# An attention and expert kernel on one core: the first pair's keys and values brought together by one-hot products on TensorE, not by gathers

## Chip, cores and metric

One core of a Trainium2 chip. The metric is the device time of one execution in microseconds. The kernel before took 506.49 us (median of three runs, 504.88 to 506.61).

## The reference

The input `x` is 2048 tokens of 128 channels. Cut to what matters here:

```python
h = layernorm(x) * (1 + ca) + sa
q, k, v = split(h @ qkv_w.T + qkv_b)                  # 16 heads of 8 channels
scores = sigmoid(sigmoid(relu(h @ r_w1.T + r_b1) @ r_w2.T + r_b2))
top_idx = top_k(scores of a head over the tokens, 819)  # k_keep = int(2048 * 0.4)
attn = q @ k.T / sqrt(8), all but the 819 kept keys of the head at -1e30
x = x + ga * (softmax(attn) @ v)
h = layernorm(x) * (1 + cb) + sb
x = x + gb * (the one of 8 experts that the router picks, for each token)
```

Each head keeps 819 of 2048 tokens as keys, and which ones is known only at run time. So the kernel has to bring the kept keys and values of a head together.

## The kernel before, in words

Engines and their queues: TensorE (`pe`), VectorE (`dve`), ScalarE (`act`), GpSimd (`pool`) and SyncE (`sp`) each run their own program in the order written, tied by semaphores.

**Start.** Layer norm, products for queries, keys, values and router scores. VectorE searches each head's threshold in 11 rounds (L977 to L987), in whose gaps TensorE makes keys and values (`KV`, copied by ScalarE at L755 and written to `kv_dram` by SyncE). Then VectorE computes for each token and head the place of the token among the kept ones (L992 to L1023), TensorE turns the table (L1454), and VectorE takes it from PSUM (L1025) and splits it in a low part and a key (L1027 to L1033).

**Lists.** Heads are worked in 8 pairs. The list of pair `i` is the row numbers of its kept keys and values in `kv_dram`. `columns(i)` (L1037) and `onehot(i)` (L1049) of VectorE make one-hot tables, `index_mm(i)` (L1459) multiplies them in 16 products, ScalarE copies (`copy_codes`), `row_to_partition(i)` (L1473) turns, and `index(i)` (L1057) writes the row numbers. `AHEAD = 5` lists, those of pairs 0 to 4, are made in front, one after another. Lists 5, 6 and 7 are made in the loop: `LIST_BESIDE` is {11: 5, 15: 6, 19: 7}; their columns are made by GpSimd (L651), their products stand in chunks 11, 15 and 19 and their row turn in the chunk behind.

**Gathers.** With a list, GpSimd issues 13 indirect DMAs of 128 rows each (L586) into `G`. For pair 0 they are split in 7 and 6, and VectorE prepares the keys (`prep`, L1071): bias added, then three bf16 parts whose sum is the key, in six copies (48 rows) beside each other in `KS`. TensorE turns them (L1600, L1609) into `KT`, where the keys of a head lie side by side, head 0 on partitions 0 to 63 and head 1 on 64 to 127. For the other pairs GpSimd does the same (L591 to L634) and TensorE turns in `turn_k` (L1523), in chunk n with n % 4 == 1.

**Lead and loop.** The tokens' queries are cut in 4 chunks of 512, so there are 32 chunks in all. A score unit (`score_unit`, L1505) is one 128-query by 410-key product, whose maximum VectorE takes from one of three PSUM banks (L1107). Of each chunk there are 16. `LEAD = 28` units, ordered by `unit_order()`, run ahead of the loop; each chunk of the loop issues 16 units of later chunks. The row maxima of a chunk, split in three parts, are turned (L1534), copied (L790) and sent by SyncE into the query rows (`m_rows`, L499); no chunk can start before its own have landed. In chunk n, TensorE makes scores (L1569) in 7 steps, ScalarE the exponentials (L823), TensorE weighs the values (L1585, L1593). After `m_rows(0)` SyncE issues the load of all experts (`WE`, two DMAs of 2 MB, L512), which waits for the lists in front since they use the same memory.

**End.** Second layer norm, router, and 23 tiles of expert work.

## Time and profile before

| | |
|---|---|
| median of three runs | 506.49 us |
| the profiled execution | 507.32 us, of which the span of the trace 505.4 us |
| TensorE busy | 435.7 us (86%) |
| VectorE busy | 399.7 us (79%) |
| ScalarE busy | 312.4 us (62%) |
| GpSimd busy | 221.9 us (44%) |
| mean granted clock of TensorE | 0.906 |

A reader sees in such a profile how long each engine had work in hand, what its idle time waited for, and a chain of work followed back from the end. A granted clock of 1.0 stands for 2.4 GHz, 0.5 for 1.2 GHz.

### The profile page before, as it was taken

To read this page: it belongs to the slowest core of one execution; us is meant where nothing else is said; L and a number is where in the kernel's file an instruction comes from. 1 tells how busy PE (TensorE), PEld (TensorE's weight loads), DVE (VectorE), ACT (ScalarE), POOL (GpSimd) and SP (SyncE) were. 2 spreads that over 40 slices of the span, in tenths; PEclk is the share of its full clock that TensorE was granted. 3 is DMA by queue.
4 is the path that set the end of the run, shared out by engine and by line. 5 is a ranking of instruction groups with operands and counts; after the bars stand their busy time and mean duration, and the time that the engine had idled before them with its cause. 6 is when DMAs were issued, how large, how long until landed. Compare 5 with 4: busy or idle time off the path is not lost.

```text
span 505.4 us, 9690 instructions
## 1 busy us (share of the span) xinstructions
PE 435.7 (86%) x3335; PEld 188.9 (37%) x3335; DVE 399.7 (79%) x1081; ACT 312.4 (62%) x486; POOL 221.9 (44%) x304
## 2 busy tenths in 40 slices
PE   3666558989999999999999999999999998599782
PEld 3332442223333333333323233323333225289672
DVE  8788958869988988789769958888888996746451
ACT  2435200367877877687667748787787874068562
POOL 3300287573505367358437625435000600177775
PEclk9888555599999999899869969999999999899997
DMA  8032610630100100010010000001000032021210
GB/s 255 1 123 66 161 13 6 227 116 5 35 2 7 35 4 6 9 32 3 6 35 3 7 24 15 5 5 36 1 2 2 2 100 68 10 77 53 63 31 23
DMA packets 20209, 21.15 MB, mean 42 GB/s; under 512 B 5740, under 2 KB 15792, under 8 KB 20160
## 3 DMA queue, kind: packets, MB, share of 16 engines
q1 hardware_dynamic: 14689, 16.13, 10.5%
q0 software_dynamic: 5168, 4.00, 3.8%
q8 instruction: 27, 0.44, 0.3%
q10 hardware_dynamic: 303, 0.40, 0.2%
q14 instruction: 22, 0.18, 0.1%
HBM read 14.42 MB, written 7.27 MB: 43 GB/s over the span
## 4 chain that ended last, share of the span: by engine, by line
PE 61%; DVE 20%; issue 7%; ACT 4%; DMA 4%; POOL 3%; POOLq 0%; SPq 0%; DVEq 0%; ACTq 0%
PE OP L1585 18%; PE ST L1569 12%; DVE tile_max L1107 8%; PE SC L1517 6%; PE SC L1515 5%; PE ST L1738 2%; PE OP L1593 2%; PE ST L1542 2%; DMA KV<-rows_dram,owner 2%; DVE PR L977 2%; PE SC L1727 2%; PE ST L1548 2%; POOL out L721 2%; ACT PR L823 1%; PE ST L1469 1%
## 5 line engine op out<-in xcount | busy, mean ns | idle before, releaser
L1107 DVE TENSOR_REDUCE tile_max<-SC 128x1 f32<-128x410 f32 (+1 forms) x512 | 268.5, 576 | 47.4 <-PE SC L1515 44.0
L823 ACT ACTIVATE PR<-ST 128x1024 f32<-128x1024 f32 (+1 forms) x224 | 210.7, 960 | 52.0 <-PE ST L1569 51.8
L586 POOL DMA_INDIRECT G<-kv_dram,idx x104 | 106.6, 1025 | 142.4 <-ACT PR L823 79.6
L1569 PE MATMUL ST<-QS,KT 51*128 51x512 bf16 (+1 forms) x416 | 116.8, 400 | 1.6 <-DMA QS<-MT 1.2
L1585 PE MATMUL OP<-PR,VS 128*32 128x512 f32 x768 | 107.8, 635 | 0.1
L1515 PE MATMUL SC<-KT,QS 48*128 48x410 bf16 x256 | 79.6, 366 | 4.0 <-ACT KT L794 1.9
L1569 PEld LDWEIGHTS ST<-QS,KT 51*128 51x128 bf16 (+1 forms) x416 | 31.7, 96 | 55.4 <-issue 41.9
L1517 PE MATMUL SC<-KT,QS 48*128 48x409 bf16 x128 | 47.1, 368 | 3.4 <-DVE tile_max L1107 0.2
L1519 PE MATMUL SC<-KT,QS 48*128 48x358 bf16 x128 | 43.5, 340 | 0.7 <-DVE tile_max L1107 0.7
L712 POOL DMA_INDIRECT KV<-rows_dram,owner x23 | 24.1, 1047 | 40.8 <-DVE owner L1351 34.1
L1515 PEld LDWEIGHTS SC<-KT,QS 48*128 48x128 bf16 x256 | 19.5, 95 | 46.1 <-DVE tile_max L1107 30.6
L1517 PEld LDWEIGHTS SC<-KT,QS 48*128 48x128 bf16 x128 | 12.0, 94 | 56.0 <-DVE tile_max L1107 42.9
L641 POOL TENSOR_TENSOR XN<-OTS,REC 128x128 f32<-128x128 f32 x14 | 5.5, 412 | 56.5 <-DVE REC L1130 52.8
L878 ACT ACTIVATE HT<-ST,mod_col,one_cb 128x128 f32<-128x128 f32 x23 | 10.5, 457 | 30.2 <-PE ST L1718 30.2
L790 ACT ACTIVATE MT<-ST 24x128 bf16<-24x128 bf16 x32 | 8.5, 267 | 31.6 <-PE ST L1548 16.5
L721 POOL DMA_INDIRECT out<-PR,owner x23 | 23.8, 1035 | 7.0 <-issue 5.8
L1369 DVE COPY PR<-WE 128x512 f32 x23 | 10.4, 453 | 20.6 <-PE ST L1738 20.5
L1738 PE MATMUL ST<-PR 128*128 128x128 f32 x184 | 24.9, 278 | 0.8 <-ACT PR L889 0.4
L1520 PE MATMUL SC<-KT,QS 48*128 48x51 bf16 x128 | 24.7, 193 | 0.0
L1727 PE MATMUL SC<-HT,PR 128*128 128x128 f32 x184 | 24.3, 276 | 0.0
L1585 PEld LDWEIGHTS OP<-PR,VS 128*32 128x32 f32 x768 | 15.4, 110 | 21.1 <-issue 15.1
L1738 PEld LDWEIGHTS ST<-PR 128*128 128x128 f32 x184 | 22.3, 191 | 1.5 <-issue 1.1
(269 smaller groups left out, 568.6 us busy)
## 6 DMA issues: line engine op xcount, KB each, us to landing
kv_dram<-KV SPq DMA_DIRECT2D x4, 512.0 KB, 2.9
WE<-in_w_fc SPq DMA_DIRECT2D x1, 2048.0 KB, 9.3
WE<-in_w_proj SPq DMA_DIRECT2D x1, 2048.0 KB, 14.7
G<-kv_dram,idx POOLq DMA_INDIRECT x104, 2.4
q_parts_dram<-QP SPq DMA_DIRECT2D x3, 512.0 KB, 3.7
QS<-q_parts_dram SPq DMA_DIRECT2D x16, 96.0 KB
X<-in_x SPq DMA_DIRECT2D x4, 256.0 KB, 5.9
QS<-q_parts_dram SPq DMA_DIRECT2D x16, 64.0 KB
```

Of the source, the lines that this page charges most:

```text
L586: pool.indirect_dma_start(G[:, i % 2, slot_of(s), :], None, kv_dram, bass.IndirectOffsetOnAxis(ap=idx[:, i, s:s + 1].bitcast(U32), axis=0) ...
L721: pool.indirect_dma_start(out[0], bass.IndirectOffsetOnAxis(ap=owner[:, n:n + 1].bitcast(U32), axis=0), YS[:, n, :], None, bounds_check=L ...
L823: nc.scalar.activation(PR[:, k, 0:cols], ST[:, (KSTEPS * n + k) % 2, 0:cols], ACT.Exp, scale=float(D) ** -0.5).then_inc(exp_done, 1)
L1107: v.tensor_reduce(tile_max[:, n % 2, at_col:at_col + 1], bank(RING_AT["unit", u])[:, 0:410 - f], AX.X, ALU.max).then_inc(s_reduced, 1)
L1515: last = mm(to[:, 0:410], q, KT[rows, i % 2, 0:410], start=True, stop=True)
L1517: last = mm(to[:, 0:409], q, KT[rows, i % 2, 410:KEEP], start=True, stop=True)
L1519: mm(to[:, 0:358], q, KT[rows, i % 2, 410:768], start=True, stop=True)
L1520: last = mm(to[:, 358:409], q, KT[rows, i % 2, 768 + GAP:KTCOLS], start=True, stop=True)
L1569: last = mm(ST[:, at_step % 2, 512 * e:512 * e + 512], KT[rows, i % 2, P * tile:P * tile + P], QS[rows, i % 2, CHUNK * c:CHUNK * (c + 1)], ...
L1585: last = mm(OP[32 * g:32 * g + 32, :], VS[:, i % 2, tile, :], PR[:, k, 512 * e:512 * e + 512], start=first, stop=False, skip_group_check=True)
L1727: last = mm(SC[:, b, P * c:P * c + P], WFC[:, b, P * c:P * c + P], HT[:, P * n:P * n + P], start=True, stop=True)
L1738: last = mm(ST[:, b, 0:E], R2[:, b, P * c:P * c + P], WPROJ[:, b, P * c:P * c + P], start=(c == 0), stop=(c == 3))
```

## The change

Pair 0 has no list and no gathers any more. GpSimd adds the bias to the keys and values of heads 0 and 1 for all 2048 tokens in SBUF and splits them in three bf16 parts (`split0`, into `parted`). VectorE compares, for each of the 16 token tiles and both heads, the 896 slot numbers (`column`, written by GpSimd at the start) with each token's place; this gives a one-hot row for each token (`hot`, a ring of 7). TensorE multiplies parts by one-hot rows, 64 products in all, summed over the tiles in two PSUM banks: each kept token's parts arrive in its slot's column. A product with `repeat` puts the parts in the six copies that `KT` wants, and seven products with `add_parts` turn and add the parts of the values.

`AHEAD` is 3. List 1 is made at the beginning of the lead by VectorE (columns, one-hot, index) with its products between units 3 to 7, list 2 at its end, with columns by GpSimd. Lists 3 to 7 are made in the loop: `LIST_BESIDE` is {3: 3, 7: 4, 11: 5, 15: 6, 19: 7}. The units run in natural order, so that chunk 0 has its 16 maxima after 16 units and not after 20. The keys of pair 1 are turned at step 5 of chunk 1 and not at step 2. The expert load waits for the products instead of five lists. The table of constants has 160 more columns. The diff, cut:

```diff
-TURN_AFTER = 7
-ODD_AFTER, ODD_TURN_AFTER = 7, 9
-AHEAD = 5
+TURN_AFTER = [0, 14] + [7] * (NP - 2)
+AHEAD = 3
+HOTS = 7
 LIST_BESIDE = {NQ * (i - 3) + 3: i for i in range(AHEAD, NP)}
...
-ORDER = unit_order()
+ORDER = [(n, qt, f, e) for n in range(NCH) for qt in range(4) for f in range(2) for e in (1, 0)]
...
-            sp.wait_ge(columns_ready, AHEAD)
+            sp.wait_ge(columns_ready, 1)
+            sp.wait_ge(hot_used, NT)
             for n, w_part in enumerate((w_fc, w_proj)):
...
+            def numbered(e, first, last, tile):
+                nc.gpsimd.tensor_tensor(column[:, e, P * first:P * last].rearrange("p (k j) -> p k j", j=P),
+                                        block[:, tile:tile + last - first, :].to_broadcast([P, last - first, P]),
+                                        lane.to_broadcast([P, last - first, P]), ALU.add).then_inc(pool_step, 1)
+                pool.wait_ge(pool_step, next_step())
+            numbered(0, 0, BLOCKS, 0)
+            numbered(1, 0, BLOCKS - 1, 1)
+            numbered(1, BLOCKS - 1, BLOCKS, 0)
+            nc.gpsimd.tensor_copy(repeat16[:, :], cc("repeat")).then_inc(pool_step, 1)
...
+            nc.gpsimd.tensor_copy(add_parts16[:, :], cc("add_parts")).then_inc(pool_step, 1)
...
+            nc.gpsimd.memset(parted, 0.0).then_inc(pool_step, 1)
...
+            nc.gpsimd.memset(parted[:, :, :, KROWS:SROWS], 1.0).then_inc(pool_step, 1)
...
+            def split0():
+                pool.wait_ge(kv_ready, NT // 2)
+                pool.wait_ge(bias_in, 16)
+                shape = [P, NT, 2, 2 * D]
+                nc.gpsimd.tensor_tensor(biased, KV[:, :, 0:4 * D].rearrange("p t (e c) -> p t e c", e=2),
+                                        BG[:, 0:1, 0:2, :].to_broadcast(shape), ALU.add).then_inc(part_step, 1)
+                pool.wait_ge(part_step, 1)
+                nc.gpsimd.tensor_copy(parted[:, :, :, 0:16], biased).then_inc(part_step, 1)
+                pool.wait_ge(part_step, 2)
+                nc.gpsimd.tensor_tensor(rest1, biased, parted[:, :, :, 0:16], ALU.subtract).then_inc(part_step, 1)
...
-            gathers(0, range(EARLY), gathered_early)
-            gathers(0, range(EARLY, STEPS), gathered_late)
-            gathers(1)
-            prep(1)
-            prep_v(1)
...
+            columns(2)
+            pool.wait_ge(columns_late, 3)
+            gathers(1)
+            prep(1)
+            prep_v(1)
             for i in range(2, NP):
                 if AHEAD <= i + 1 < NP:
                     columns(i + 1)
...
-            for i in range(AHEAD):
-                copy_codes(i)
-            act.wait_ge(ktr_odd, 1)
-            nc.scalar.activation(KT[64:128, 0, :], OP[:, :].bitcast(BF16)[64:128, 0:KTCOLS], ACT.Copy)\
-                .then_inc(kt_odd, 1)
+            act.wait_ge(hot_used, NT)
+            nc.scalar.activation(turned0[:, 0:512], SC[:, 0, :], ACT.Copy).then_inc(turned0_ready, 1)
+            act.wait_ge(kt0_done, 1)
+            nc.scalar.activation(KT[:, 0, 0:512], ST[:, 1, 0:512], ACT.Copy).then_inc(kt0_ready, 1)
+            copy_codes(1)
...
-            v.tensor_copy(place_int[:, :], MP[:, 0:CT]).then_inc(dve_step, 1)
+            v.tensor_copy(places, MP[:, 0:CT]).then_inc(dve_step, 1)
+            dve.wait_ge(dve_step, next_step())
+            dve.wait_ge(init_pool, 1)
+            for t in range(NT):
+                if t >= HOTS:
+                    dve.wait_ge(hot_used, t - HOTS + 1)
+                for e in range(2):
+                    v.tensor_scalar(hot[:, t % HOTS, e, :], column[:, e, :], places[:, H * t + e:H * t + e + 1], None,
+                                    ALU.is_equal).then_inc(hot_ready, 1)
+            v.tensor_copy(place_int[:, :], places).then_inc(dve_step, 1)
...
+            dve.wait_ge(hot_used, NT)
+            v.tensor_copy(turned0[:, 512:KTCOLS], SC[:, 2, 0:KTCOLS - 512]).then_inc(turned0_ready, 1)
...
+            dve.wait_ge(kt0_done, 1)
+            v.tensor_copy(KT[:, 0, 512:KTCOLS], ST[:, 1, 512:KTCOLS]).then_inc(kt0_ready, 1)
...
-            for i in range(AHEAD):
-                columns(i)
-                onehot(i)
-                if i >= 1:
-                    index(i - 1)
-            index(AHEAD - 1)
+            columns(1)
+            onehot(1)
...
+            units(0, 8)
+            index(1)
+            units(8, LAST[0] + 4)
+            onehot(2)
+            units(LAST[0] + 4, LEAD)
+            index(2)
...
-            for i in range(AHEAD):
-                index_mm(i)
-                row_to_partition(i)
+            pe.wait_ge(parted_ready, 1)
+            for t in range(NT):
+                of_t = NT // CHUNKS * (t % CHUNKS) + t // CHUNKS
+                for half, (c0, c1) in enumerate(((0, 512), (512, KTCOLS))):
+                    for e in range(2):
+                        if half == 0:
+                            pe.wait_ge(hot_ready, 2 * t + e + 1)
+                        last = mm(SC[64 * e:64 * e + 64, 2 * half, 0:c1 - c0], parted[:, of_t, e, :],
+                                  hot[:, t % HOTS, e, c0:c1], start=(t == 0), stop=(t == NT - 1), skip_group_check=True)
+                last.then_inc(hot_used, 1)
+            pe.wait_ge(turned0_ready, 2)
+            mm(ST[:, 1, 0:512], repeat16[:, :], turned0[:, 0:512], start=True, stop=True)
+            mm(ST[:, 1, 512:KTCOLS], repeat16[:, :], turned0[:, 512:KTCOLS], start=True, stop=True).then_inc(kt0_done, 1)
...
+            index_ready(1)
+            for u in range(3, 8):
+                if u < 6:
+                    index_part(1, [range(0, 5), range(5, 10), range(10, NT)][u - 3])
+                score_unit(u)
+            row_to_partition(1)
+            for k in range(7):
+                last = mm(ST[:, 1, 32 * k:32 * k + 32], turned0[:, P * k:P * k + P], add_parts16[:, :], start=True, stop=True)
...
-                    if k == 2 and n % NQ == 1 and n // NQ + 1 < NP:
+                    if k == (5 if n == 1 else 2) and n % NQ == 1 and n // NQ + 1 < NP:
                         turn_k(n // NQ + 1)
```

## Rows read from the trace of the kernel before

**Rows 1.** The page: clock row of the 40 slices, and the chain's shares by engine
```profile
PEclk9888555599999999899869969999999999899997
...
PE 61%; DVE 20%; issue 7%; ACT 4%; DMA 4%; POOL 3%; POOLq 0%; SPq 0%; DVEq 0%; ACTq 0%
```
**Rows 2.** Windows: stretch, its length, busy of each engine, clock, DMA share, GB/s
```profile
65.00:70.00 5.00, 4.10 (x47) 3.50 (x45) 2.59 (x4) 0.43 (x2) 4.05 (x3) 0.50 0.08 10
...
50.95:76.34 25.39, 14.09 (x171) 11.57 (x170) 18.60 (x34) 3.51 (x9) 13.25 (x11) 0.52 0.36 81
76.34:92.65 16.31, 14.00 (x43) 3.95 (x44) 14.92 (x36) 1.18 (x2) 12.47 (x13) 0.50 0.07 8
92.65:105.70 13.05, 11.73 (x58) 2.88 (x58) 9.79 (x25) 6.79 (x8) 6.32 (x16) 0.59 0.92 324
```
**Rows 3.** The chain in order of time, 45 to 108 us: start, length, what
```profile
55.90 2.06 PE SC L1469 x16
...
68.71 1.00 POOL G L586
...
76.91 3.53 DVE tile_max L1107 x7
...
99.78 5.91 DMA QS<-MT
105.74 0.39 PE ST L1569
```
**Rows 4.** Timeline of ScalarE: the copy of a pair's keys, pairs 2 to 6
```profile
148.60 0.91 ACT L794 ACTIVATE KT<-SC 128x896 bf16<-128x896 bf16 x1
...
186.86 0.91 ACT L794 ACTIVATE KT<-SC 128x896 bf16<-128x896 bf16 x1
...
228.46 0.91 ACT L794 ACTIVATE KT<-SC 128x896 bf16<-128x896 bf16 x1
...
272.73 0.91 ACT L794 ACTIVATE KT<-SC 128x896 bf16<-128x896 bf16 x1
...
317.07 0.91 ACT L794 ACTIVATE KT<-SC 128x896 bf16<-128x896 bf16 x1
```
**Rows 5.** Timeline, 30 to 56 us: the last copy of keys and values
```profile
39.01 0.60 ACT L755 ACTIVATE KV<-SC 128x512 f32<-128x512 f32 x1 [1.46 <-PE SC L1424]
```
**Rows 6.** Timeline at 227 us, and the durations of L1121 (minimum, median, maximum)
```profile
227.07 1.69 POOL L659 TENSOR_TENSOR B<-key_of,C 128x896 f16<-128x896 f16 x1
...
227.65 1.13 DVE L1121 TENSOR_TENSOR NM<-NM 128x8 f32<-128x8 f32 x1
...
L1121 DVE TENSOR_TENSOR NM<-NM x32: 153/157/1129, 89.2 to 401.0; 128x8 f32<-128x8 f32 x32
```
**Rows 7.** Groups: a GpSimd addition over 208 elements, a cast over 512
```profile
L603 POOL TENSOR_TENSOR G<-G,BG 128x208 f32<-128x208 f32 x7 | 4.3, 620 | 15.4 <-DMA G<-kv_dram,idx 15.4
...
L567 POOL CAST place<-C 128x512 f16<-128x512 f32 x1 | 0.6, 609 | 0.1
```
**Rows 8.** Timeline and durations of VectorE: steps that bound the comparison
```profile
50.13 0.29 DVE L1023 TENSOR_SCALAR PR<-PR 128x256 f32<-128x256 f32 x1
...
48.64 0.41 DVE L1016 TENSOR_SCALAR PR<-PR,offsets,need 128x256 f32<-128x256 f32 x1
...
L1053 DVE TENSOR_TENSOR ABUF<-place,lo_of x8: 682/684/685, 55.1 to 289.9; 128x1024 f16<-128x1024 f16 x8
...
52.93 1.09 DVE L1040 TENSOR_TENSOR WE<-key_of,C 128x896 f16<-128x896 f16 x1
...
8.38 1.12 DVE L923 TENSOR_SCALAR XN<-X,mv,rstd 128x128 f32<-128x128 f32 x4
```
**Rows 9.** Timeline of TensorE: four weighings, and one unit at half and full clock
```profile
225.66 0.61 PE L1585 MATMUL OP<-PR,VS 128*32 128x512 f32 x4
...
78.53 0.52 PE L1517 MATMUL SC<-KT,QS 48*128 48x409 bf16 x1
...
206.03 0.34 PE L1517 MATMUL SC<-KT,QS 48*128 48x409 bf16 x1
```

More of the change, by code:

```diff
@@ L87, in ring_table @@
         for j in range(UPC):
-            if j == TURN_AFTER and n % NQ == 1 and n // NQ + 1 < NP:
+            if n % NQ == 1 and n // NQ + 1 < NP and j == TURN_AFTER[n // NQ + 1]:
                 ring.append(("turn", n // NQ + 1))
@@ L143, in constants @@
     cols["sum_groups"] = (p[:, None] % 32 == np.arange(32)[None, :])
+    repeat = np.zeros((P, P))
+    add_parts = np.zeros((P, 32))
+    for e in range(2):
+        for part, row, n in ((0, 0, 3), (1, 3, 2), (2, 5, 1)):
+            for d in range(D):
+                repeat[64 * e + 16 * part + d, [64 * e + D * (row + k) + d for k in range(n)]] = 1
+                add_parts[64 * e + 16 * part + D + d, 16 * e + d] = 1
+        for j in range(PARTS):
+            repeat[64 * e + KROWS + j, 64 * e + KROWS + j] = 1
+        add_parts[64 * e + KROWS, 16 * e + D] = 1
+    cols["repeat"] = repeat
+    cols["add_parts"] = add_parts
     cols["number"] = P * np.arange(NT)[None, :] + p[:, None] + 1
@@ L232, in build @@
         A1 = ABUF[:, 0:1024].bitcast(FP16).rearrange("p (b e q t) -> p b e q t", b=2, e=2, q=ROWS)
-        B0 = WE.rearrange("p n c -> p (n c)")[:, 0:AHEAD * NT * CODES].bitcast(FP16)\
-            .rearrange("p (i t e c) -> p i t e c", i=AHEAD, t=NT, e=2)
+        WEF = WE.rearrange("p n c -> p (n c)")
+        B0 = WEF[:, 0:NT * CODES].bitcast(FP16).rearrange("p (t e c) -> p t e c", t=NT, e=2)
+        column = WEF[:, 448:448 + KTCOLS].bitcast(FP16).rearrange("p (e c) -> p e c", e=2)
+        hot = WEF[:, 1408:1408 + HOTS * KTCOLS].bitcast(BF16).rearrange("p (s e c) -> p s e c", s=HOTS, e=2)
+        repeat16 = sb("repeat16", [P, P], BF16)
+        add_parts16 = sb("add_parts16", [P, 32], BF16)
         by_code = sb("by_code", [2 * CODES, 2, 2 * ROWS])
@@ L258, in build @@
         place_int, lo_int, key_int = [work[:, 10 + n, :].bitcast(I32) for n in range(3)]
+        places = flat[:, 3328:3584]
+        parted = flat[:, 3584:4608].bitcast(BF16).rearrange("p (t e c) -> p t e c", t=NT, e=2)
+        biased, rest1, rest2 = [flat[:, 4608 + 512 * n:5120 + 512 * n].rearrange("p (t e c) -> p t e c", t=NT, e=2)
+                                for n in range(3)]
+        turned0 = flat[:, 6144:6144 + KTCOLS // 2].bitcast(BF16)
         OS = sb("OS", [P, 512])
@@ L575, in _, with gathers @@
+            split0()
             pool.wait_ge(kv_out, 16 * 4)
             pool.wait_ge(bias_in, 16)
-            def gathers(i, tiles=range(STEPS), fetched=gathered):
-                pool.wait_ge(idx_ready, i + 1)
+            def gathers(i):
+                pool.wait_ge(idx_ready, i)
                 if i >= 2:
@@ L582, in gathers @@
                     pool.wait_ge(o_norm, 2 * (i - 2))
-                for s in tiles:
+                for s in range(STEPS):
                     if i >= 2:
@@ L837, in _ @@
                     copy_sum(n - 1)
-                if n % NQ == 1 and n // NQ + 1 < NP:
+                if n % NQ == 1 and 2 <= n // NQ + 1 < NP:
                     copy_kt(n // NQ + 1)
@@ L852, in _ @@
                 weights(n, 5, 4)
+                if n == 1:
+                    copy_kt(1)
                 weights(n, 6, 4)
@@ L1457, in _, with index_ready, index_part @@
                 q_rest(2, g)
-            def index_mm(i):
-                if i < AHEAD:
-                    pe.wait_ge(columns_ready, i + 1)
-                else:
-                    pe.wait_ge(columns_late, 3 * (i - AHEAD + 1))
-                pe.wait_ge(onehot_ready, i + 1)
-                if i >= 2:
-                    pe.wait_ge(code_copied, i - 1)
-                for t in range(NT):
+            def index_ready(i):
+                if i == 1:
+                    pe.wait_ge(columns_ready, 1)
+                else:
+                    pe.wait_ge(columns_late, 3 * (i - 1))
+                pe.wait_ge(onehot_ready, i)
+            def index_mm(i):
+                index_ready(i)
+                index_part(i, range(NT))
+            def index_part(i, tiles):
+                for t in tiles:
                     last = mm(tokens_of(i)[0], B1[:, i % AHEAD, t, :, :].rearrange("p e c -> p (e c)"), A1[:, i % 2, :, :, t],
                               start=(t == 0), stop=(t == NT - 1), skip_group_check=True)
-                last.then_inc(idx_mm, 1)
+                if NT - 1 in tiles:
+                    last.then_inc(idx_mm, 1)
             def row_to_partition(i):
-                pe.wait_ge(code_copied, i + 1)
-                if 2 <= i < AHEAD:
-                    pe.wait_ge(idx_ready, i - 1)
+                pe.wait_ge(code_copied, i)
                 to_row = cc("to_row").rearrange("p (e w s) -> p e w s", e=2, w=GROUPS)
```

159 lines of the change are left out of this document (67 added, 92 removed).

## The prediction

> **What bounds the kernel now.** I read the clock row and the chain of the page first. The chain is 61% TensorE and 20% VectorE. TensorE's clock stands at its lower level in slices five to eight, about 50 to 101 us, the stretch that the change rebuilds [rows 1]. The windows say the same: clock 0.52, 0.50 and 0.59 (1.0 is 2.4 GHz, 0.5 is 1.2 GHz) in three stretches: lists and gather, lead (the 28 score units ahead of the loop), chunk 0 [rows 2]. The chain through them [rows 3] runs list 0 (its 16 products at 55.90), seven gathers that GpSimd issues one after another up to the last (68.71), their landing, the keys' split and turn, then from 76.91 VectorE's maxima at about 0.50 each (seven in 3.53), the start of the loop at 92.65 [rows 2], and the row maxima of chunk 1, whose transfer takes 5.91 us behind the 4 MB expert load; chunk 1 starts at 105.74. From there TensorE paces a loop of 32 chunks.
>
> Where a list lies beside a chunk is seen in that loop. The key copy comes once per pair of heads, so its starts time a pair [rows 4]: 148.60 to 186.86 is 38.26 us with no list; the three pairs that follow, each with one list, take 41.60, 44.27 and 44.34. A list in the loop costs 3.3, 6.0 and 6.1 us. Its products take 2.06 us [rows 3] and its row turn 0.5; the rest is mostly the clock, which has its dips behind the three: 8 tenths in slice 17 (202 to 215 us), 8 and 6 in slices 20 and 21, 6 in slice 24 [rows 1].
>
> **The loop.** Lists 3 and 4 move from the front into chunks 3 and 7, which TensorE paces as it does chunks 11, 15 and 19. Two lists at 3.3 to 6.1 are +6.7 to +12.2 us; I take the mean of three, 15.4 / 3 = 5.1, twice: **+10.3**. Nothing hides them, since that engine has no idle time there. GpSimd's steps for them (columns, index) queue ahead of the gathers of pairs 2 and 3, about 6 us of columns each; the gathers are paced by exponentials anyway, and pair 2's keys, ready near 135 by 13 gathers at 1.3 each from 111, are wanted near 146. At nothing, with 11 us of cover.
>
> **The front, step by step.**
> *Start and search.* The constants grow by 160 columns, 80 KB on 678; GpSimd gets some 6 us of set-up, up to about 24 us; together +0.5 (0 to 2). GpSimd's six steps that split keys and values (512 elements each) start when the last keys are copied, at 39.6 [rows 5]. Additions: 208 elements take 0.62, 896 take 1.69, so 512 about 1.1; casts 0.61 [rows 7]: three of each and the gaps are 5.5 us, over the last rounds of VectorE's search, now bare of GpSimd work. VectorE's 8-element subtraction, 0.157 us as a rule, took 1.13 beside GpSimd's 1.69 and ended with it [rows 6]. So small SBUF steps of the search will be held; none held is 0, all held 5.5. Each of three rounds has two short ones, and the selection behind has two scans: I take **2.0**. (The Trainium skill, SBUF: State Buffer, "SBUF: two separate sides", says that the pair of ports is an exclusive lock against two-input and two-port steps; by it the counts, one input at one element a cycle, would go free and the term would be near 2 rather than 5.5; [rows 6] agree for a two-input step.) Places are then ready at 51.4 + 2.5 = 53.9.
> *One-hot rows.* 32 VectorE comparisons of 896 fp16 elements with a per-partition scalar. No row has that form. A 256-element fp32 step takes 0.29 with a constant, and 0.41 with two per-partition scalars: two elements a cycle of 0.96 GHz, 0.15 fixed, 0.06 a scalar. A two-input fp16 step reaches two a cycle as well (1024 in 0.68), or only one if an operand is repeated inside (896 in 1.09) [rows 8]. If the two gains multiply, 896 take 0.23 + 0.21 = 0.44, and 0.36 from start to start (four normalising steps of 128 elements and two scalars, 0.34 each by that count, span 1.12, so they start 0.26 apart, 0.08 less than they take): 32 x 0.36 = 11.7. At two a cycle it is 19, at one 34. I take four a cycle: both gains stand in rows, and the operand is contiguous. (The Trainium skill, VectorE: DVE Perf Modes, "The perf-mode tier table", gives four for a 16-bit tensor with a scalar; no run here shows it yet.)
> *Products.* 64, in two column groups, one a head. Four 512-column fp32 products in column groups took 0.61 together [rows 9], so I let the heads run side by side. 409 columns take 0.52 at half clock and 0.34 at full, so they stream in 0.36 and 0.18; 896 in 0.79 and 0.39. Sixteen tiles are 12.6 at half clock, 6.3 at full. VectorE and half-clock TensorE are about level; with the start and the last tile I end the stage at 53.9 + 13.1 = 67.0.
> *Back to keys.* Copy (ScalarE 0.7), two products (0.9), copy (0.7): 69.4. The query rows are no limit: the DMA engines' share is 0.08 from 65 on [rows 2], so they have landed.
> *VectorE before the first maximum.* Columns and one-hot of list 1: 1.1 + 1.1 + 0.7 = 2.9 after 69.2. GpSimd's columns of list 2 (1.69, 2.46, 1.69) begin in the same moment and can hold each: 0 to 5.8. The hold of [rows 6] was 1.0; I take 1.5, one and a half of it. First maximum at **73.6**, before 76.91.
> *Lead.* 28 maxima at 0.50 are 13.9, the split of the row maximum 0.5, two index steps 0.4, a one-hot 0.7: 15.5. TensorE takes 32 list products (4.1 us), two row turns (1.0) and seven products for the values (0.7) between units at half clock, and has about 0.15 us to spare in each of 28 and two banks in store: 1.0 to 2.4 us show, I take 1.8, and 0.4 for the last row turn. The loop starts at **91.3**, before 92.65. Removed by this: 13 of 26 gathers (GpSimd), both splits (2 x 1.7 of VectorE), three lists.
> *Chunk 0.* Before, 13.05: 11.73 busy at mostly half clock [rows 2], 11.9 with its gaps, and 1.2 for the transfer. The expert load now follows the 16th maximum with 12 units behind, not the 20th with 8, so it starts 4 us earlier against the loop and that wait goes; what is late next is TensorE itself. 91.3 + 11.9 = 103.2 against 105.74: **-2.5**. Key copy 1, moved from the middle of chunk 1 to its end, is 0.91 of ScalarE in either place [rows 4]; its keys are ready near 104, wanted near 110; at nothing, up to +1 if exponentials slip.
>
> Sum: 507.32 (the profiled execution; span 505.4) - 2.5 + 10.3 = 515.1. That execution lies 0.83 over the median of the three, so 514.3.
>
> **Rivals.**
> *A, the stage of one-hot rows is longer.* VectorE at two a cycle (19 - 11.7 = +7.4), or the heads one after another at half clock (25 for 12.6, +12, less if the clock rises). For it: no row of this form. Against: both gains and the column groups are in rows. With the first, 521.7.
> *B, faster, by the clock.* The dense products lift the clock at about 55 and it stays up: chunk 0 takes 10 rather than 11.9, the lead loses 0.8 less, the stage ends with VectorE 1 us earlier, and nothing is held (3.5); that is 7.2 more. Lists 3 and 4 cost only their products and turn, 2.7 each: 5.4. Net -9.7 + 5.4 = -4.3: 502.2. It decides where a list costs under 3.5. Against: behind lists the clock fell, and in the lead VectorE sets the pace, at which TensorE stayed at half clock.
> *C, no change.* The holds are not there and the early lists are like the first (3.3 each): -2.5 - 3.5 + 6.7, about 507; the clock's chance alone separates it from the forecast.
>
> **How the numbers follow.** Forecast 0.57, A 0.17, B 0.11, C 0.15. The predicted time is the forecast's, 514.3. The range, 505 to 521, leaves out most of B and the tail of A. This kernel's time tells nothing under 0.5% (2.5 us) from no change. Faster 0.11; within, C and the forecast's lower edge, 0.17; slower 0.72.
>
> **What would show it.** Right: two more pairs of 41.6 to 44.3 between key copies; comparisons 0.36 apart; search steps of 1 us beside GpSimd at 40 to 45; chunk 1 starting near 103. Wrong: comparisons 0.6 or more apart (A); clock 1.0 from 56 to 100 (B); pairs with lists under 41 (B, C). The forecast fails most easily at the price of a list early in the loop, and at the clock that the new stage leaves behind.

## The result, and the profile after

| | median, us | all of its runs | profiled execution: time, span, mean clock |
|---|---|---|---|
| before (beside the change) | 505.69 | 502.23 to 506.61 (4) | 507.32, 505.4, 0.906 (the one of the page) |
| after | 519.87 | 514.55 to 522.51 (4) | 514.55, 512.7, 0.901 |

The change makes the kernel slower: the ratio of the times is 1.026, interval 1.016 to 1.036. Medians here and below are of all executions of a kernel, ratios leave out those over 1.5% above its fastest. The forecast was 514.3 (range 505 to 521) and slower; the median lies 1.1 us below the upper end of the range. The sum had been made for a profiled execution, 515.1, and the profiled execution of the changed kernel took 514.55, but that is the fastest of its four.

Below, a dip is a stretch of the loop in which TensorE's granted clock stands at its lower level, a unit is one of the 128-query score products ahead of the loop's chunks, and a list's products are its 16 products on TensorE.

The page of the changed kernel, clock row and the chain's shares by engine, beside [rows 1]:

```profile
PEclk9876975599699999879969989999999997899997
...
PE 63%; DVE 22%; issue 5%; ACT 3%; DMA 2%; POOL 2%; POOLq 0%; DVEq 0%; ACTq 0%
```

Of the four slices at 5 tenths in a row before (about 50 to 101 us) two are left. In exchange there are more slices under 9 tenths behind them. The windows of the changed kernel (stretch, length, busy time of PE, PEld, DVE, ACT, POOL, clock, DMA share, GB/s), as in [rows 2]:

```profile
39.95:54.06 14.11, 9.81 (x21) 3.73 (x23) 12.69 (x45) 6.34 (x10) 5.39 (x6) 0.64 0.14 45
54.06:69.05 14.99, 12.92 (x69) 4.24 (x69) 14.85 (x41) 4.25 (x8) 0.48 (x1) 1.00 0.60 152
69.05:90.00 20.95, 15.04 (x88) 6.18 (x88) 17.47 (x32) 1.29 (x6) 13.99 (x11) 0.53 0.17 50
90.00:103.00 13.00, 12.67 (x82) 3.80 (x83) 10.88 (x25) 6.79 (x8) 7.48 (x11) 0.58 0.72 255
...
125.00:130.00 5.00, 4.76 (x37) 2.71 (x33) 3.67 (x11) 2.27 (x5) 2.98 (x3) 0.83 0.05 7
130.00:135.00 5.00, 5.00 (x30) 1.09 (x29) 2.36 (x6) 2.54 (x5) 2.92 (x8) 0.50 0.01 1
135.00:140.00 5.00, 5.00 (x31) 1.33 (x30) 3.08 (x6) 3.00 (x4) 0.06 (x1) 0.65 0.27 82
170.00:190.00 20.00, 19.50 (x180) 7.51 (x178) 16.79 (x39) 14.48 (x24) 8.73 (x15) 1.00 0.10 24
```

The new stage runs at full clock from 54 to 69, and the clock is back at its lower level for the lead. List 3 is made at 127: there the clock falls for ten microseconds. Around list 4 (chunk 7, 170 to 190) it does not fall at all.

The pairs, by ScalarE's copy of a pair's keys, as in [rows 4]; and the copy of a chunk's output, chunks 0 to 2 of the changed kernel (its last three rows), since the first key copy has moved within its chunk:

```profile
152.08 0.91 ACT L859 ACTIVATE KT<-SC 128x896 bf16<-128x896 bf16 x1
192.38 0.91 ACT L859 ACTIVATE KT<-SC 128x896 bf16<-128x896 bf16 x1
236.44 0.91 ACT L859 ACTIVATE KT<-SC 128x896 bf16<-128x896 bf16 x1
280.72 0.91 ACT L859 ACTIVATE KT<-SC 128x896 bf16<-128x896 bf16 x1
322.56 0.91 ACT L859 ACTIVATE KT<-SC 128x896 bf16<-128x896 bf16 x1
360.82 0.91 ACT L859 ACTIVATE KT<-SC 128x896 bf16<-128x896 bf16 x1
...
105.08 0.60 ACT L866 ACTIVATE OS<-OP 128x512 f32<-128x512 f32 x1
115.66 0.60 ACT L866 ACTIVATE OS<-OP 128x512 f32<-128x512 f32 x1
124.95 0.60 ACT L866 ACTIVATE OS<-OP 128x512 f32<-128x512 f32 x1
```

Before, the output copy of chunk 0 stood at 108.22:

```profile
108.22 0.60 ACT L801 ACTIVATE OS<-OP 128x512 f32<-128x512 f32 x1
...
146.47 0.60 ACT L801 ACTIVATE OS<-OP 128x512 f32<-128x512 f32 x1
```

So the front gives 108.22 - 105.08 = 3.1 us. Then, against a pair of 38.26 without a list: the first four chunks with list 3 take 44.88 (the output copy of chunk 4 is at 149.96) where before took 38.25, +6.6; the pairs with lists 4 to 7 take 40.30, 44.06, 44.28 and 41.84, +2.0, +5.8, +6.0, +3.6. Five lists together cost 24.1 us where three cost 15.4 before [rows 4]: +8.7. The part behind the loop, called the tail here, is 1.7 longer (90.65 from the last output copy against 88.91; its first two slices are at 7 and 8 tenths of the clock instead of 9 and 8). -3.1 + 8.7 + 1.7 = +7.3, the difference of the spans, 512.7 - 505.4.

### The profile page after: what moved, and what is told of

The parts are those of the page before. It is cut to its first block, busy times and chain, and to the rows that moved or that the text cites. A ratio compares the mean times of both kernels' runs of the same rounds, so it can differ in the third digit from the quotient of the medians.

```text
span 512.7 us, 9755 instructions
## 1 busy us (share of the span) xinstructions
PE 449.4 (88%) x3358; PEld 192.3 (38%) x3362; DVE 408.9 (80%) x1085; ACT 313.1 (61%) x491; POOL 237.8 (46%) x317
## 3 DMA queue, kind: packets, MB, share of 16 engines
q1 hardware_dynamic: 14689, 16.21, 10.3%
## 4 chain that ended last, share of the span: by engine, by line
PE 63%; DVE 22%; issue 5%; ACT 3%; DMA 2%; POOL 2%; POOLq 0%; DVEq 0%; ACTq 0%
PE OP L1645 18%; PE ST L1627 13%; DVE tile_max L1154 7%; PE SC L1574 6%; PE SC L1572 5%; PE ST L1517 3%; PE OP L1653 2%; DMA KV<-rows_dram,owner 2%; DVE WE L1101 2%; PE ST L1798 2%; DVE PR L1045 2%; PE ST L1599 2%; PE ST L1605 2%; PE SC L1787 2%; ACT PR L888 1%
## 5 line engine op out<-in xcount | busy, mean ns | idle before, releaser
L642 POOL DMA_INDIRECT G<-kv_dram,idx x91 | 91.9, 1010 | 94.1 <-ACT PR L888 71.7
L1627 PE MATMUL ST<-QS,KT 51*128 51x512 bf16 (+1 forms) x416 | 118.3, 404 | 0.4 <-ACT PR L888 0.3
L1645 PE MATMUL OP<-PR,VS 128*32 128x512 f32 x768 | 109.3, 643 | 0.1
L1645 PEld LDWEIGHTS OP<-PR,VS 128*32 128x32 f32 x768 | 15.5, 110 | 21.5 <-issue 15.4
```

The costliest lines, as they stand in the source:

```text
L642: pool.indirect_dma_start(G[:, i % 2, slot_of(s), :], None, kv_dram, bass.IndirectOffsetOnAxis(ap=idx[:, i, s:s + 1].bitcast(U32), axis=0) ...
L1627: last = mm(ST[:, at_step % 2, 512 * e:512 * e + 512], KT[rows, i % 2, P * tile:P * tile + P], QS[rows, i % 2, CHUNK * c:CHUNK * (c + 1)], ...
L1645: last = mm(OP[32 * g:32 * g + 32, :], VS[:, i % 2, tile, :], PR[:, k, 512 * e:512 * e + 512], start=first, stop=False, skip_group_check=True)
```

## The experiments

In each run the kernel before was timed on the same chip; ratios are to that. "Output copy" stands for the rows of the output copy above, which time chunks: 9.3 us for a chunk, 10.4 for the one with a key copy.

**The same kernel once more.**

> The changed kernel once more, unedited. Its profiled execution took 514.55 us, 7.2 more than that of before, but its fast runs stood 13 us over those of before. Theory 1 (the clock behind each list lasts differently long from run to run): times between 514 and 523 again, and the profile's five pairs with a list cost other amounts than 6.6, 2.0, 5.8, 6.0 and 3.6 us, each at least 2.0. Theory 2 (something outside the lists differs from run to run, for instance the front): the start of the loop moves by 3 us or more from 91.9, and the pairs stay as they were.

518.83 (514.99 to 520.14), ratio 1.017 (1.009 to 1.024). The profiled execution, 520.14, has its first output copy at 107.01 and not 105.08, and its five lists cost 6.1, 5.6, 5.8, 3.5 and 5.6: 26.7 and not 24.1. List 4 had its dip this time. The loop starts at 91.93, as in the first profile (91.87); the later output copy comes from chunk 0, where the clock is at 0.50 up to 106 here and was at 0.75 from 100 and 1.00 from 102 there. Executions of one kernel differ by where the clock falls, some 5 us from one to the next, so from here on the rows of stretches weigh more than a few microseconds of total.

**The two lists taken out of the loop.** Pairs 3 and 4 gather by list 2, so their part of the output is left out; the lists of pairs 5 to 7 stay where they are. The edit, cut (the waits that count lists follow it):

```diff
-LIST_BESIDE = {NQ * (i - 3) + 3: i for i in range(AHEAD, NP)}
+LIST_BESIDE = {11: 3, 15: 4, 19: 5}
+LIST_OF = {1: 1, 2: 2, 3: 2, 4: 2, 5: 3, 6: 4, 7: 5}
```

> The changed kernel without lists 3 and 4: pairs 3 and 4 gather by the rows of list 2, so that their part of the output is not computed; lists for pairs 5, 6 and 7 stay in chunks 11, 15 and 19. Theory 1 (the loss is the two lists in the loop): the pairs of chunks 1 to 9 take 38.3 us each, and the time falls by 8 to 12 us under the changed kernel, to about that of before less 3 (the front's gain), 503 to 509. Rival (the front's GpSimd holds and the later key copy carry the loss): it falls by less than 5 us.

502.44 (500.1 to 506.46), ratio 0.990 (0.986 to 0.994): 16.4 us under the repeated kernel, 5.8 under before. The first output copy is at 104.31 and the first four chunks take 37.9; the three lists that are left cost 3.4, 7.0 and 5.7. The front alone is a gain, and two lists in the loop are more than the whole loss. The fall is more than the 8 to 12 us expected, and not all of it is the lists' own. Of the 17.0 between the two profiled executions (518.3 and 501.3), 12.2 stand in the two pairs, 2.7 before the first output copy, 3.3 in the tail, and the three lists that are left cost 1.2 more.

**The other half alone: the kernel before with lists 3 and 4 moved into the loop.**

```diff
-AHEAD = 5
+AHEAD = 3
```

> The kernel before with lists 3 and 4 moved into chunks 3 and 7 and nothing else (AHEAD 3, pair 0 still gathered). Theory 1: slower than before by two lists in the loop, 4 to 12 us, less what two lists fewer in front give back. In front the gathers and not the lists end last, so that is 0 to 2 us: 509 to 517. Rival (lists 3 and 4 cost little in the loop and the loss came with the one-hot stage): within 3 us of before.

517.96 (515.87 to 522.13), ratio 1.016 (1.009 to 1.024): 9.7 us over before. The output copy of chunk 0 is at 106.03, 2.2 us earlier, as two lists fewer are made in front; the five pairs with lists take 46.7, 44.0, 44.3, 44.2 and 41.8. That is just over the 509 to 517 expected. This one constant does nearly what the whole change did to the time. So by medians the front of the change is worth about -6, and two more lists in the loop +16 by the run before this one and +12 by this one (9.7 and the 2.2 gained in front). By the rows of the profiled executions the two pairs cost 12.2 and 14.1 (8.4 + 5.7), and the tail is 2.8 longer here too, with the old front.

**The list's 16 products spread, four at a time among the loop's other products.**

```diff
-                        unit()
-                        unit()
                         if n in LIST_BESIDE:
+                            unit()
                             pe.wait_ge(sum_copied, n)
-                            index_mm(LIST_BESIDE[n])
+                            index_ready(LIST_BESIDE[n])
+                            index_part(LIST_BESIDE[n], range(0, 4))
+                            unit()
+                            index_part(LIST_BESIDE[n], range(4, 8))
...
+                    if k == 4 and n in LIST_BESIDE:
+                        index_part(LIST_BESIDE[n], range(8, 12))
                     unit()
...
+                            index_part(LIST_BESIDE[n], range(12, 16))
```

> The changed kernel with the 16 products of each list in the loop not in one run but four at a time, behind the two units of step 3, the first scores of step 4 and the unit behind them. Theory 1a (the clock falls because 16 small products stand in one run of 2.0 us): the clock stays at 1.0 behind most lists, each list costs 2 to 3 us, and the time falls by 8 to 15 us under the changed kernel. Theory 1b (the clock falls for the work that a list adds, wherever it stands in the chunk): dips as before, times within 3 us of the changed kernel.

519.44 (516.59 to 523.43), ratio 1.019 (1.011 to 1.026): no gain. The pairs with lists 4 to 7 take 43.3, 44.9, 44.8 and 43.4, so there is a dip at each. So it isn't that the products stand in one piece. That left the question what in a list lets the clock fall, and the next view put it more sharply. TensorE in the changed kernel around list 3:

```profile
126.26 0.39 PE L1627 MATMUL ST<-QS,KT 115*128 115x512 bf16 x1
126.58 0.34 PE L1574 MATMUL SC<-KT,QS 48*128 48x409 bf16 x1
126.68 0.34 PE L1572 MATMUL SC<-KT,QS 48*128 48x410 bf16 x1
126.95 2.04 PE L1517 MATMUL ST<-ABUF,B 128*56 128x64 f16 x16
128.93 0.60 PE L1627 MATMUL ST<-QS,KT 51*128 51x512 bf16 x1
128.93 0.52 PE L1572 MATMUL SC<-KT,QS 48*128 48x410 bf16 x1
```

Sixteen products of 64 columns are 1024 columns, and they take 2.04 us. A unit of 410 columns takes 0.34 before them and 0.52 behind them: the clock goes down while they run. 1024 columns in 2.04 us are 0.5 a nanosecond; the 64 products of the new stage, of 512 or 384 columns each, ran at full clock. The moving operand of a list's product is `A1[:, i % 2, :, :, t]`: 64 fp16 elements, each 32 bytes behind the last.

**One product of the sixteen.** In this run and the next two, pairs 3 to 7 gather by list 2, so that their part of the output is left out. The edit, cut:

```diff
             def index_part(i, tiles):
+                if i >= AHEAD:
+                    tiles = tiles[-1:]
```

> The changed kernel, but each list in the loop (3 to 7) makes 1 of its 16 products of 56 rows by 64 columns; the one-hots, the copies, the turn of the row and the transfers stay. Pairs 3 to 7 gather by list 2, so that their keys are not those of the reference. Theory 1 (TensorE's clock falls on the list's products, which took 2.04 us from 126.95 and had the clock at one half from 128 to 138): without the products no fall, each list is nearly free, so 5 lists give back 4 to 6 us each where they fell, and the time is about that without lists 3 and 4 and less: 495 to 502. Theory 2 (it falls for what else the list brings: VectorE's one-hot of 1.1 us, the row's turn, the copies): dips stay, each list chunk at 12 to 15 us instead of 9.3, time 514 to 520.

494.64 (492.47 to 495.19), ratio 0.974 (0.966 to 0.982). The pairs with lists 4 to 7 take 38.6 to 38.7, +0.4 each, and no dip stands behind a list. So it is the products; VectorE's one-hot, the copies, the row's turn and the transfers don't do it. Two dips are left in the loop. One is in chunk 25 (11.7 us for 10.4), where no list is made. The other is in chunk 4 (12.3 us), a chunk behind list 3, and it stands behind another wait, for VectorE, which is held in a small step in the split of the row maximum (the chain):

```profile
136.64 1.60 DVE NM L1168
```

**Sixteen products that read neighbours.**

```diff
+                    hot_rows = A1[:, i % 2, :, :, t]
+                    if i >= AHEAD:
+                        hot_rows = A1[:, i % 2].rearrange("p e q t -> p (e q t)")[:, 2 * ROWS * t:2 * ROWS * (t + 1)]
```

> The changed kernel, but the moving operand of the 16 products of each list in the loop is read from 64 neighbouring fp16 elements (128 bytes) instead of 64 elements 32 bytes apart; the products' number, size and outputs' shapes stay, the numbers are not the lists', and pairs 3 to 7 gather by list 2. Theory 1a (the products are slow because of how their columns are read, 2.04 us for 1024 columns, and the slow reading lets the clock fall): the 16 products take 0.5 to 1 us, the clock stays at 1.00, time 495 to 505. Theory 1b (their number and their small size do it, whatever the reading): the products take 1.5 to 2 us, dips as before, time 514 to 520.

495.14 (493.23 to 499.9), ratio 0.979 (0.969 to 0.989). TensorE at list 3, the windows behind it, and the durations of the 112 list products (minimum, median, maximum; the 32 of lists 1 and 2 still read as before), first of this run:

```profile
126.86 0.65 PE L1520 MATMUL ST<-ABUF,B 128*56 128x64 f16 x16
127.45 0.39 PE L1630 MATMUL ST<-QS,KT 51*128 51x512 bf16 x1
127.45 0.34 PE L1575 MATMUL SC<-KT,QS 48*128 48x410 bf16 x1
...
125.00:130.00 5.00, 4.76 (x53) 1.90 (x49) 4.35 (x12) 3.61 (x8) 2.98 (x3) 1.00 0.05 7
130.00:135.00 5.00, 4.89 (x45) 1.51 (x43) 4.48 (x9) 4.13 (x5) 3.02 (x9) 1.00 0.30 83
...
L1520 PE MATMUL ST<-ABUF,B x112: 193/193/298, 73.7 to 284.9; 128*56 128x64 f16 x112
```

and of the changed kernel:

```profile
L1517 PE MATMUL ST<-ABUF,B x112: 275/297/298, 73.7 to 302.1; 128*56 128x64 f16 x112
```

The same number of products, of the same size, into the same place: 0.65 us and not 2.04, 193 ns and not 297 each, and the clock stays. A pair with a list takes 38.9 to 39.0, +0.65. Nearly the whole cost of a list in the loop was the step of 32 bytes: 1.4 us (2.04 - 0.65) as the slow reading itself, the rest of the 3.5 to 6 as the dip behind it. (The Trainium skill, Advanced Engine Details and Errata, "SBUF Cachelines", has a line of 16 bytes that wants at least two hits for full speed; at 32 bytes each element has a line of its own, and the two durations agree with that.) Chunk 4 has the same wait for VectorE as in the run before (1.61 us in the chain), but here no dip follows it (1.00 from 136 to 144) and the chunk takes 11.1, not 12.3; so such a wait doesn't always end in one.

**Twice as many products that read neighbours.**

```diff
+                tiles = [(t, 0) for t in tiles] + [(t, 1) for t in tiles if i >= AHEAD]
```

> The run with neighbouring elements again, but each list in the loop makes 32 products instead of 16 (each tile twice; pairs 3 to 7 gather by list 2). Theory 1a (slow reading makes the clock fall, not small products as such): 32 products take 1.2 to 1.4 us, no dip, pair pitch 39.3 to 40, time 497 to 501. Theory 1b (a stretch of small products of some length is enough): at 1.3 us in some lists the clock falls, pitches of 41 to 44 among them, time 502 to 515.

497.22 (495.94 to 500.39), ratio 0.981 (0.976 to 0.987). In this run:

```profile
126.87 1.12 PE L1521 MATMUL ST<-ABUF,B 128*56 128x64 f16 x32
...
125.00:130.00 5.00, 4.77 (x66) 2.19 (x64) 4.33 (x11) 3.37 (x8) 2.99 (x3) 1.00 0.08 7
```

Thirty-two take 1.12 us, a pair with a list 39.4 in three of the four (40.0 in one), no dip behind a list. So it isn't the count of small products that brings the clock down. That it is the slow reading, and not just 2 us of small products whatever they read, is argued from this and from the spread list: no run had small products that read neighbours for as long as 2 us.

**The layout done properly, in both kernels.** The one-hots of the rows are laid out tile, head, row instead of head, row, tile; the lists are the real ones. The edit of the changed kernel, cut:

```diff
-        A1 = ABUF[:, 0:1024].bitcast(FP16).rearrange("p (b e q t) -> p b e q t", b=2, e=2, q=ROWS)
+        A1 = ABUF[:, 0:1024].bitcast(FP16).rearrange("p (b t e q) -> p b t e q", b=2, e=2, q=ROWS)
...
-                shape = [P, 2, ROWS, NT]
+                shape = [P, 2, NT, ROWS]
...
-                    last = mm(tokens_of(i)[0], B1[:, i % AHEAD, t, :, :].rearrange("p e c -> p (e c)"), A1[:, i % 2, :, :, t],
+                    last = mm(tokens_of(i)[0], B1[:, i % AHEAD, t, :, :].rearrange("p e c -> p (e c)"), A1[:, i % 2, t, :, :],
```

> The changed kernel with the whole result kept: the one-hots of the rows are laid out tile by tile, so that each product of a list reads 64 neighbouring fp16 elements. VectorE writes them with the place as the inner, repeated operand (at least the 0.68 us of before, at most 1.1 us). Theory 1a (the clock falls through the strided reading): the 16 products of a list take 0.6 to 0.8 us, a pair with a list in the loop takes 38.6 to 39.4 us, no stretch at half clock after 107, time 493 to 499. Rival (the keys of the measured lists and the gathers by list 2 had to do with it, that is the data): dips stay in part, 500 to 515.

> The kernel before with the same layout of the row one-hots: it says what the change is worth when a list costs little. Theory 1a: its three lists in the loop (44.0, 43.9 and 41.8 us a pair in the profile of before) fall to 38.6 to 39.4, that is 12 to 15 us less; five lists ahead of the loop are faster by some tenths each: time 490 to 495. Then the change in front (first weighted products 3.1 us earlier) should make the changed kernel with this layout the faster of the two by 0 to 4 us; the prediction's own view, that a list in the loop costs 3 to 6 us as such, gives the kernel before the advantage by 5 us or more.

The changed kernel: 498.63 (497.81 to 500.2), ratio 0.982 (0.978 to 0.986). The kernel before: 502.62 (497.36 to 506.23), ratio 0.989 (0.985 to 0.992). Both are faster than the kernel before and the changed one, and their order has turned round: with cheap lists the change is ahead by 4.0 us of median, though the runs of the two overlap. The kernel before missed its forecast of 490 to 495. Its three lists gave back 10.3 us of the 12 to 15 expected (one dip is left, in chunk 9, where no list is made), and its front, which was to gain some tenths, lost 2.8. Part of that is the layout's own price: VectorE's one-hot, whose repeated operand is now the inner one, takes 1.22 us instead of 0.68 (the row of the changed kernel):

```profile
L1136 DVE TENSOR_TENSOR ABUF<-place,lo_of x7: 1210/1216/1217, 72.7 to 284.7; 128x1024 f16<-128x1024 f16 x7
```

In the kernel before, five of these lie in front, in the open (5 x 0.54 = 2.7 us; its first output copy comes at 111.0 against 108.2), in the changed one or two do. What the change itself is worth with cheap lists is therefore some 2 us of those 4, and its sign is less sure than that of the layout. Pairs with lists take 39.4 to 39.6 here, not 38.9, by the same 0.5. One chunk of the profiled changed kernel, chunk 1, took 13.6 and not 10.4, with the clock down from 109 to 117; no list stands there, only a wait of TensorE of 0.94 us for VectorE ahead of it.

**The writes apart instead of the reads.** The last run tried to save that half microsecond, with VectorE walking as it does now and only its output going to the new places; GpSimd's wait of a run below is in it too:

```diff
-                v.tensor_tensor(A1[:, i % 2, :, :, :], place16[:, :, :].rearrange("p q (a t) -> p a q t", a=1).to_broadcast(shape),
+                v.tensor_tensor(A1[:, i % 2, :, :, :].rearrange("p t e q -> p e q t"), place16[:, :, :].rearrange("p q (a t) -> p a q t", a=1).to_broadcast(shape),
```

> The changed kernel with its whole result and two edits: (1) the row one-hots are laid out tile by tile as in the run g1_after_rows, but VectorE still walks them with the tile innermost, so that its writes lie 128 bytes apart and its reads are those of before; (2) GpSimd starts its columns of list 2 only after VectorE's one-hot of list 1, as in the run f4_pool_waits. Theory A (VectorE's 0.68 us hangs on its operands' inner step, not on that of its output): the one-hot stays at 0.68 us, a pair with a list takes 38.9 us instead of 39.5, and the front is 1 to 3 us earlier; time 493 to 497. Theory B (the output's step counts too): 1.1 to 1.3 us, pairs 39.4 to 39.6, time 495 to 499.

540.95 (538.34 to 543.76), ratio 1.065 (1.061 to 1.070): a miss, 42 us above what either theory allowed. Of this run:

```profile
L1137 DVE TENSOR_TENSOR ABUF<-place,lo_of x7: 4700/4721/4721, 70.7 to 319.9; 128x1024 f16<-128x1024 f16 x7
...
129.37 4.72 DVE L1137 TENSOR_TENSOR ABUF<-place,lo_of 128x1024 f16<-128x1024 f16 x1
...
136.32 1.05 PE L1518 MATMUL ST<-ABUF,B 128*56 128x64 f16 x16
...
130.00:135.00 5.00, 1.08 (x14) 0.33 (x10) 5.00 (x5) 1.47 (x2) 3.71 (x1) 0.82 0.02 2
135.00:140.00 5.00, 5.00 (x42) 1.83 (x34) 3.17 (x8) 2.26 (x6) 1.09 (x2) 0.50 0.03 3
```

A VectorE step of 1024 fp16 elements takes 0.68 us with its output in order and 4.72 with its writes 128 bytes apart, 4.6 ns each. TensorE then waits (1.08 us busy in five), and behind the wait the clock falls as it did behind the slow reads; a pair with one of lists 4 to 7 takes 45.2 to 47.8. So a long wait of TensorE and a slow operand end in the same dip. That the two have one cause is argued, not shown. The row of TensorE has a second use: it is the list's 16 products reading neighbours at half clock, 1.05 us, where they take 0.65 at full clock.

**The two holds in front.** First GpSimd without its split during the search (pair 0 has zeros for keys and values):

```diff
-            split0()
+            pool.sem_inc(parted_ready, 1)
```

> The changed kernel without GpSimd's split of keys and values during the search (pair 0 has zeros for them). Theory of the prediction: VectorE's small operations in the search are held by GpSimd's operations of 0.7 to 1.3 us; without the split the copy of the places starts at 51.9 instead of 54.06 (2.2 us earlier), and with it the stage of the one-hots and the first unit (69.05 to 66.9). Rival: the places are late by the longer init on GpSimd before 39 us; then only some tenths come back. Loop start earlier by 2 us at most; time 512 to 520, which can't tell 2 us alone.

513.96 (513.19 and 514.72), ratio 1.014 (1.003 to 1.024). The copy of the places starts at 52.18 and not 54.06, the first score unit at 67.17 and not 69.05, the loop at 89.98 and not 91.87: 1.9 us, passed on whole up to the start of the loop. By the output copy of chunk 0 only 0.25 is left (104.83 against 105.08), since in this execution the clock stayed down longer in chunk 0. The search with the split (the changed kernel: VectorE, then GpSimd beside it) shows who holds whom:

```profile
40.28 0.47 DVE L1045 TENSOR_SCALAR_CACHE_REDUCE PR<-scores_r,candidate 128x256 f32<-128x256 f32 x1
40.68 0.08 DVE L1045 DVE_READ_ACCUMULATOR PR<-scores_r,candidate 128x1 bf16 x1
40.68 1.23 DVE L1048 TENSOR_SCALAR next_from<-C,candidate 128x4 f32<-128x4 f32 x1
...
46.96 0.23 DVE L1048 TENSOR_SCALAR next_from<-C,candidate 128x4 f32<-128x4 f32 x1
...
40.63 1.26 POOL L616 TENSOR_TENSOR PR<-KV,BG 128x512 f32<-128x512 f32 x1 [15.72 <-ACT KV L814]
```

The count over 256 elements is not held; the step of four elements behind it lasts until GpSimd's addition ends, at 1.23 against 0.23.

Then GpSimd's columns of list 2 made to wait for VectorE's one-hot of list 1:

```diff
+            pool.wait_ge(onehot_ready, 1)
             columns(2)
```

> The changed kernel, but GpSimd starts its columns of list 2 only when VectorE's one-hot of list 1 is done. Prediction's step: VectorE's two operations on the columns of list 1 (2.42 and 1.70 us beside GpSimd) take 1.12 each, the first maximum starts 1.5 to 2 us earlier than 73.47. Rival: list 2 comes later by as much, so that unit 28 and the loop start at 91.9 don't move or move back by up to 1 us. Time 514 to 520.

512.96 (505.2 to 518.22), ratio 1.004 (0.996 to 1.012), against 1.017 of the repeated kernel on another chip; the medians of all executions, 512.96 and 507.48, make it 1.011. VectorE at the columns of list 1, in the changed kernel:

```profile
68.79 2.42 DVE L1123 TENSOR_TENSOR WE<-key_of,C 128x896 f16<-128x896 f16 x1
71.24 1.70 DVE L1128 TENSOR_TENSOR B<-WE,C 128x896 f16<-128x896 f16 x1
...
73.47 2.04 DVE L1154 TENSOR_REDUCE tile_max<-SC 128x1 f32<-128x410 f32 x4
```

and with the wait:

```profile
68.34 1.08 DVE L1124 TENSOR_TENSOR WE<-key_of,C 128x896 f16<-128x896 f16 x1
69.46 1.09 DVE L1129 TENSOR_TENSOR B<-WE,C 128x896 f16<-128x896 f16 x1
...
71.07 2.05 DVE L1155 TENSOR_REDUCE tile_max<-SC 128x1 f32<-128x410 f32 x4
```

From the columns to the first maximum 2.73 us and not 4.68: the hold was 1.95. The loop starts at 89.48 and not 91.87; list 2, whose columns now end at 77.4 and not 75.3, was not late. The rival that list 2 takes it back falls. Whether the time of the whole kernel gained as much can't be said: the runs lie 13 us apart, by the clock.

## Why the prediction was right

*Direction and size.* Its sum, -2.5 + 10.3, was measured as -3.1 + 8.7 in the profiled execution, with 1.7 more from the tail, which the sum did not have. 515.1 against 514.55 is thus partly luck: the loop term was 1.6 too high there and the tail missing. By the medians, 514.3 against 519.87, the sum was 5.6 too low; the repeated kernel's profile has 11.3 for the loop (26.7 - 15.4), a front of -1.2 and a tail of +2.8. By the medians of the runs that part the two terms, the front was worth -5.8 and the two lists +16.4 or +11.9: both terms were too small, with opposite signs, so part of what they missed cancelled.

*The loop.* The forecast took 5.1 a list from three pairs that ran from 3.3 to 6.1 [rows 4]. The two lists added cost 6.6 and 2.0 in one execution and 6.1 and 5.6 in the other; between profiles with and without them the two pairs differ by 12.2 and 14.1. Its bounds for the two, 6.7 to 12.2, held in the changed kernel's own profiles (8.6 and 11.7); the medians, at 16.4, went beyond them, with the tail and chunk 0 in it. That "the rest is mostly the clock" held too; what the forecast called the price of a list was the price of reading it at a step of 32 bytes. It had the row that says so, 16 products in 2.06 us at half clock in front [rows 3], and carried it into the loop as it stood. There, where they begin at full clock, they took 2.04 all the same (297 ns each in both places). Reading neighbours, they took 1.05 us at half clock and 0.65 at full. That two clocks give one duration is a sign that the engine waits for its operand.

*GpSimd's steps in the loop, costed at nothing,* cost something, by a way the text did not name. Its columns of list 4 start at 141.12 in chunk 4, and beside them a subtraction of 8 elements in the split of the row maximum takes 1.17 us; TensorE's turn of that maximum waits for it. The chain of the changed kernel:

```profile
141.79 1.09 DVE NM L1171
142.88 0.04 issue
142.92 0.23 PE ST L1591
```

Chunk 4 takes 10.1 and not 9.3; with one product of sixteen it is the 1.60 and the dip shown there. It is the hold of [rows 6] in a new place, 0.8 us, within the 6.6 of list 3. In the chain this is the term that the forecast put at nothing with 11 us of cover: it had looked at when the columns are due, not at what they hold.

*Start and search.* The places were forecast to be copied by 53.9 (51.4 + 2.5); the copy starts at 54.06 and takes 0.42, so it ends at 54.48, 3.1 later than before and not 2.5. Of that, 0.9 came before the last copy of keys and values (39.95 against 39.01; 0.5 forecast) and 2.2 by the split (2.0 forecast; 1.9 came back without it). (The Trainium skill, SBUF: State Buffer, "SBUF: two separate sides", which the forecast cited, names as held the steps with two SBUF inputs and those in a two-port mode; the counts, which the forecast took for neither, are free. A one-input step of four fp32 elements was held too, at 1.23 in the row above; no run shows whether it ran in a two-port mode.)

*One-hot rows.* 444 ns each and 0.36 apart were forecast as 0.44 and 0.36; the two gains multiply:

```profile
L1101 DVE TENSOR_SCALAR WE<-WE,PR x32: 441/444/453, 54.5 to 65.8; 128x896 bf16<-128x896 f16 x32
...
55.18 11.66 PE L1541 MATMUL SC<-WE,PR 128*64 128x512 bf16 x64
```

The 32 one-hots span 11.7 us, from 54.52 to 66.22 (the forecast's 32 x 0.36 is 11.5, which it wrote as 11.7), with the products beside them, the last ending 0.6 us behind the last one-hot; the end, forecast for 67.0, is 66.84. Rival A had no ground. The step beneath was wrong in one respect that cost nothing: TensorE was at full clock here (1.00 in 54.06 to 69.05), not at half, and so waited 7.2 us for VectorE, which set the pace alone.

*Keys, first maximum, lead, chunk 0.* Keys ready 69.05 (69.4); hold 1.95 (1.5, and 1.95 is by the run that removed it); first maximum 73.47 (73.6); loop start 91.87 (91.3), the lead 0.7 longer than the forecast's 17.7; chunk 1 at 102.60 (103.2), chunk 0 shorter by 1.2 since the clock came up in it; in the repeated kernel, where it didn't, chunk 0 took 12.0, the forecast's 11.9. The front has several terms that each missed by up to a microsecond and cancelled.

*Rival B.* It wanted the clock to stay up behind the dense stage and lists at under 3.5. The first half happened only as long as the stage ran: TensorE then waited for VectorE (to 73.7, for list 1's columns and one-hot) and the lead was at 0.53. The second is what the layout brought about, with lists at 0.65 to 1.3: 498.63, where that rival had 502.2. It was the right condition, and nothing in the change brought it about.

*Rival C* fell with the pairs at 44.

Still open: why the clock falls behind one list and not behind another of the same kernel (list 4 in two executions), and why the tail is 1.7 to 2.8 us longer in the changed kernel. No run was made for the tail. It doesn't come from the new stage, since the kernel before with `AHEAD = 3` has it at 91.7 us, nor always from five lists in the loop, since the run in which GpSimd waits has it at 88.5.

## What to carry to other kernels

Before a step is priced at "what it costs elsewhere in this kernel", compare its columns with its time: 16 products of 64 columns in 2 us, at either clock, are an operand read badly and not a price of the step. Laying the operand out so that TensorE reads neighbours made a list fall from 3 to 6 us to 0.65 (1.2 to 1.3 with the real lists, VectorE's slower one-hot included), and was worth 3.5% in the changed kernel (ratio 0.982 after 1.017), more than the change cost; but do it where the producer can still write in order, since VectorE paid 4.0 us for writes 128 bytes apart and 0.5 for a repeated inner operand. And where one engine's work moves past another's, ask of GpSimd's steps which small VectorE step on the chain they stand beside.

## What the runs showed of the hardware

- TensorE's moving operand at a step of 32 bytes (fp16): 16 products of 64 columns take 2.04 us in a loop at full clock and 2.06 at half clock, 297 ns each; with neighbours they take 0.65 us at full clock, 193 ns each, and 1.05 at half.
- In a loop where TensorE is busy all but a few per cent, its clock fell to half behind 2 us of such products in most cases, for about ten microseconds behind list 3; a list with the fall cost 3.3 to 7.0 us in most places (8.4 at most), one without it 2.0. It did not fall behind 1.12 us of 32 small products that read neighbours, and it did behind a wait for VectorE that left TensorE 1.08 us of work in five.
- VectorE, two fp16 inputs, 1024 elements: 0.68 us in order, 1.22 with one input repeated innermost, 4.72 with the output 128 bytes apart.
- VectorE, fp16 to bf16 with a per-partition scalar, 896 elements: 0.44 us, 0.36 apart.
- A VectorE step of 4 or 8 fp32 elements lasts until the GpSimd step beside it ends (1.23 and 1.17 us for 0.23 and 0.16), while counts with an accumulator over 256 elements are not held.
